# Attention scores as four 32-row matmul tiles into four shared PSUM banks, in place of one 96-row matmul on packed operands

## The reference

```python
xn = _layernorm(x, axis=-1)
x = x + attention(xn) + ffn(xn)

# attention: 16 heads of 16, segments of 512 rows, every 8th row is a key
qkv = einsum('bmd,ed->bme', x, Wqkv)              # q is scaled by hd ** -0.5
scores = einsum('bhspd,bhskd->bhspk', q4, k4)     # 512 queries x 64 keys in each segment
c = max(scores, over blocks of 64 queries)        # one value per key and block
w = exp(scores - c)
den = sum(w, axis=-1) + 1e-10
out = (w @ v4) / den ; out @ Wout.T

# ffn
h = relu(xn @ W1 + b1)                            # 256 -> 1024
y = h @ W2 + b2                                   # 1024 -> 256
```

## Time and profile before

| | |
|---|---|
| median of 3 runs | 1187.57 us (1187.46 to 1188.78) |
| span of the profiled execution | 1189.4 us, 22871 instructions |
| PE busy | 1162.9 us (98%) |
| DVE busy | 885.6 us (74%) |
| ACT busy | 657.1 us (55%) |
| POOL busy | 613.5 us (52%) |
| hardware DMA queue | 75376 packets, 101.90 MB |
| HBM read, written | 22.16 MB, 16.78 MB |

### The profile page before, as it was taken

The page is one execution under the profiler, slowest core; times in us unless marked ns, Lnnn a source line. Parts: engine busy times, 40 slices in busy tenths (PEclk is TensorE's granted clock), DMA queues, the critical chain, the costliest instruction groups (busy, mean ns, idle before and its releaser), DMA issues.

```text
span 1189.4 us, 22871 instructions
## 1 busy us (share of the span) xinstructions
PE 1162.9 (98%) x7457; PEld 955.7 (80%) x7457; DVE 885.6 (74%) x1437; ACT 657.1 (55%) x1142; POOL 613.5 (52%) x488
## 2 busy tenths in 40 slices
PE   5799999999999999999999999999999999999998
PEld 3578888888878888888888888888888888888888
DVE  7788777778787777777777787777877777777762
ACT  4545555565655565555565555556555555555653
POOL 2435654465554455554556544556544556544554
PEclk9889999999999999999999999999999999999999
DMA  5423343222333322333222433223343233332210
GB/s 184 99 73 93 85 106 100 63 82 70 101 101 84 80 72 81 98 106 84 68 81 75 106 101 84 72 70 88 101 106 82 56 87 84 106 102 55 67 49 36
DMA packets 75402, 102.24 MB, mean 86 GB/s; under 512 B 13808, under 2 KB 42096, under 8 KB 75376
## 3 DMA queue, kind: packets, MB, share of 16 engines
q1 hardware_dynamic: 75376, 101.90, 32.6%
HBM read 22.16 MB, written 16.78 MB: 33 GB/s over the span
## 4 chain that ended last, share of the span: by engine, by line
PE 96%; DVE 1%; issue 0%; SPq 0%; POOL 0%; DMA 0%; ACT 0%; DVEq 0%; POOLq 0%
PE y_bank L690 39%; PE h_bank L690 38%; PE misc L811 5%; PE s_bank L742 5%; PE misc L814 5%; PE misc L756 2%; PE misc L690 2%; PE misc L781 0%; PE misc L764 0%; DMA q_pack<-q_hi 0%; PE s_bank L690 0%; DVE w_exp L589 0%; DVE s_max L583 0%; DVE xn_keys L544 0%; DVE w_lo L506 0%
## 5 line engine op out<-in xcount | busy, mean ns | idle before, releaser
L338 POOL TENSOR_TENSOR h_lo<-h_full,h_hi 128x512 fp32r<-128x512 f32 x256 | 336.7, 1318 | 557.2 <-ACT h_full L403 553.3
L409 ACT ACTIVATE w_exp<-w_exp 128x512 f32<-128x512 f32 x256 | 162.7, 636 | 238.7 <-DVE w_exp L589 238.7
L690 PE MATMUL y_bank<-w_hi,h_hi 128*128 128x256 f32 x1024 | 290.6, 284 | 0.0
L690 PE MATMUL y_bank<-w_lo,h_hi 128*128 128x256 f32 x1024 | 290.5, 284 | 0.0
L690 PE MATMUL y_bank<-w_hi,h_lo 128*128 128x256 f32 x1024 | 290.2, 283 | 0.0
L596 DVE RECIPROCAL den<-den 128x256 f32<-128x256 f32 x128 | 222.3, 1739 | 39.9 <-ACT den L422 39.9
L401 ACT ACTIVATE h_hi<-h_bank,b_cols 128x512 fp32r<-128x512 f32 x256 | 176.1, 688 | 82.6 <-PE h_bank L690 76.8
L690 PE MATMUL h_bank<-xt_hi,w_hi 128*128 128x512 f32 x512 | 210.8, 412 | 1.9 <-DVE q_lo L611 1.9
L690 PEld LDWEIGHTS y_bank<-w_lo,h_hi 128*128 128x128 f32 x1024 | 196.0, 191 | 9.9
L690 PEld LDWEIGHTS y_bank<-w_hi,h_hi 128*128 128x128 f32 x1024 | 195.5, 191 | 9.3
L690 PE MATMUL h_bank<-xt_lo,w_hi 128*128 128x512 f32 x512 | 201.9, 394 | 0.0
(11 more groups left out here) (91 smaller groups left out, 1708.1 us busy)
## 6 DMA issues: line engine op xcount, KB each, us to landing
q_pack<-q_hi SPq DMA_DIRECT2D x256, 128.0 KB, 2.4
x_raw<-x SPq DMA_DIRECT2D x32, 512.0 KB, 3.3
q_pack<-q_lo SPq DMA_DIRECT2D x128, 128.0 KB, 2.4
out<-y SPq DMA_DIRECT2D x32, 512.0 KB, 2.9
k_pack<-k_hi SPq DMA_DIRECT2D x256, 32.0 KB, 1.9
k_pack<-k_lo SPq DMA_DIRECT2D x128, 32.0 KB, 1.9
x_keys<-x SPq DMA_DIRECT2D x16, 128.0 KB, 3.0
w_exp<-w SPq DMA_DIRECT2D x2, 1024.0 KB, 8.8
```

The source lines that it names most:

```text
L338: pool.tensor_tensor(h_part[1][:, i % HBUF], h_full[:, i % HBUF], f32(h_part[0][:, i % HBUF]), ALU.subtract).then_inc(h_lo, 1)
L409: act.activation(w_exp[:, pair], w_exp[:, pair], ACT.Exp).then_inc(w_ready, 1)
L690: mm = pe.matmul(ps, stationary[a], moving[b], start=start and c == 0 and n == 0, stop=stop and c == len(pairs) - 1 and n == 2, skip_group ...
```

## The change

The `misc` banks and the packed buffers go. There are four `s_bank`s, and they also hold the transposes of x (banks 0 and 1), keys and values (3 and 2), and weighted values (2 and 3 for the first four pairs, 0 and 1 for the others). Scores are made for four pairs at a time, in two groups in a step: four matmuls of 32 rows, one in each block of 32 partitions and each into its own bank, hi x hi, then four hi x lo, then four lo x hi, accumulating in PSUM. The order of the work on PE, ACT and DVE is changed to suit; POOL's is not touched.

```diff
-    PAIR_ORDER = [half * (PAIRS // 2) + j for j in range(PAIRS // 2) for half in range(DH)]
-    PACKED = 16 * 6
+    GROUP = PAIRS // DH
...
-        q_pack = sb("q_pack", [P, PAIRS, SEG], F32R)
-        k_pack = sb("k_pack", [P, PAIRS, P], F32R)
...
-        misc = [bank(f"misc{i}") for i in range(2)]
         h_bank = [bank(f"h_bank{i}") for i in range(2)]
-        s_bank = [bank(f"s_bank{i}") for i in range(2)]
+        s_bank = [bank(f"s_bank{i}") for i in range(GROUP)]
+        xt_bank = s_bank[0:2]
+        pv_bank = [s_bank[2:4], s_bank[0:2]]
+        key_bank = (s_bank[3], s_bank[2])
...
@@ sync: the whole of pack(s), with its 24 DMAs and their waits, goes @@
-                if norm:
-                    pack(s)
...
@@ scalar, step @@
                 for i in range(LAG, NH - 1):
-                    if i == 3 and norm and par == 0:
-                        keys_hi(s)
                     if attention:
                         exponential(s, i - LAG)
                     if i in first:
                         hidden(past(s), first[i])
                     if i == 5 and ffn:
                         attention_hi(s, 0, par)
+                if norm and par == 0:
+                    keys_hi(s)
                 if norm:
                     transposed_hi(s, par)
...
@@ vector, step @@
-                for n in range(PAIRS):
-                    if n == 0 and keys:
-                        normalise_keys(s + 2)
-                    if n == 4 and keys:
-                        drain_kv(s)
-                    if n == 5 and keys:
-                        mask_k(s)
-                    if n == 6 and norm:
-                        transposed_lo(s, par)
+                for n in range(GROUP):
                     if attention:
                         shift_scores(s, n)
-                    if n == 1 and norm:
-                        normalise(s + 2, par)
-                    if n == 1 and keys:
-                        keys_lo(s)
-                    if n in (2, 4) and ffn:
-                        invert_den(s, RP // QUADS + n // 2 - 1)
+                if keys:
+                    normalise_keys(s + 2)
+                if norm:
+                    normalise(s + 2, par)
+                if ffn:
+                    invert_den(s, 2)
+                for n in range(GROUP, PAIRS):
+                    if attention:
+                        shift_scores(s, n)
+                if keys:
+                    keys_lo(s)
+                if norm:
+                    transposed_lo(s, par)
+                if keys:
+                    drain_kv(s)
+                if ffn:
+                    invert_den(s, 3)
+                if keys:
+                    mask_k(s)
                 if norm:
                     finish_projections(s, par)
...
@@ tensor @@
-            def scores(s, n):
-
-                pair = PAIR_ORDER[n]
-                if n % 2 == 0:
-                    pe.wait_ge(pair_packed[n // 2], (s + 2) * PACKED)
-
-                pe.wait_ge(s_shifted, past((s + 1) * PAIRS + n - 1))
-                pe.matmul(s_bank[n % 2][:], k_pack[0:PR, pair], q_pack[0:PR, pair], start=True,
-                          stop=True).then_inc(s_psum, 1)
+            def scores(s, half, par):
+
+                pe.wait_ge(k_ready, s + 2 + par)
+                pe.wait_ge(k_hi, s + 2)
+                pe.wait_ge(k_lo, s + 2)
+                pe.wait_ge(q_hi, (s + 1) * DH + half + 1)
+                pe.wait_ge(q_lo, (s + 1) * DH + half + 1)
+                if half == 0:
+                    pe.wait_ge(num_ready, past((s + 1) * QUADS))
+                    pe.wait_ge(den_ready, past((s + 1) * QUADS))
+                else:
+                    pe.wait_ge(s_shifted, (s + 1) * PAIRS + GROUP)
+                for n, (a, b) in enumerate(((0, 0), (0, 1), (1, 0))):
+                    for j in range(GROUP):
+                        rows = slice(PW * j, PW * (j + 1))
+                        mm = pe.matmul(s_bank[j][:], k_part[a][rows, half], q_part[b][rows, half],
+                                       start=n == 0, stop=n == 2)
+                        if n == 2:
+                            mm.then_inc(s_psum, 1)
...
             def transpose_x(s, par):
                 pe.wait_ge(xn_ready, s + 3)
-                pe.wait_ge(num_ready, past((s + 1) * QUADS))
-                pe.wait_ge(den_ready, past((s + 1) * QUADS))
...
+                pe.wait_ge(s_shifted, past((s + 1) * PAIRS + GROUP + 2))
...
             def transpose_keys(s):
                 pe.wait_ge(xn_keys_ready, s + 4)
-                pe.wait_ge(den_ready, past((s + 1) * QUADS))
+                pe.wait_ge(s_shifted, past((s + 2) * PAIRS))
...
@@ weighted_values @@
-                if quad == 0 and norm:
+                if quad == 0 and norm and par == 0:
+                    pe.wait_ge(k_ready, s + 4)
+                if quad == 1 and norm:
                     pe.wait_ge(xt_lo, (s + 3) * DH)
-                else:
-                    pe.wait_ge(num_ready, (s + 1) * QUADS + quad)
-                    pe.wait_ge(den_ready, (s + 1) * QUADS + quad)
...
@@ tensor, step @@
                 if attention:
-                    scores(s, 0)
-                    scores(s, 1)
+                    scores(s, 0, par)
                 for i in range(LAG, NH):
-                    if i == 3 and norm and par == 0:
+                    if i == 4 and attention:
+                        scores(s, 1, par)
+                    if i == NH - 1 and norm and par == 0:
                         transpose_keys(s)
-                    if i == 5 and norm and par == 0:
-                        keys_values(s)
-                    if i == 6 and norm and par == 0:
-                        transpose_k(s)
                     if i == NH - 1 and norm:
                         transpose_x(s, par)
                     if i in first:
                         first_product(past(s), first[i], par if ffn else 1 - par)
-                    if attention and i > LAG:
-                        scores(s, i - 1)
                     if i in second:
                         second_product(past(s), second[i])
+                if norm and par == 0:
+                    keys_values(s)
                 if ffn:
                     second_product(s, NH - 2)
-                if attention:
-                    scores(s, NH - 1)
+                if norm and par == 0:
+                    transpose_k(s)
                 if norm:
                     for m in range(DH):
                         queries(s, par, m)
```

More of the change, by code:

```diff
@@ L171, in ln_attention_ffn @@
         q_lo = sem("q_lo")
-        pair_packed = [sem(f"pair_packed{j}") for j in range(PAIRS // 2)]
         v_ready = sem("v_ready")
@@ L271, in first_step @@
                 load_x(1, 1)
[L272 to L292, removed]
             def step(s, par, ffn, attention, norm, load):
@@ L406, in exponential @@
             def exponential(s, n):
-                pair = PAIR_ORDER[n]
                 act.wait_ge(s_shifted, (s + 1) * PAIRS + n + 1)
-                act.activation(w_exp[:, pair], w_exp[:, pair], ACT.Exp).then_inc(w_ready, 1)
+                act.activation(w_exp[:, n], w_exp[:, n], ACT.Exp).then_inc(w_ready, 1)
             def attention_hi(s, quad, par):
@@ L420, in attention_drain @@
                 act.wait_ge(att_ready, past(n - QUADS))
-                act.copy(num[:, quad], misc[0][:]).then_inc(num_ready, 1)
-                act.add(den[:, quad], misc[1][:], GUARD).then_inc(den_ready, 1)
+                act.copy(num[:, quad], pv_bank[quad][0][:]).then_inc(num_ready, 1)
+                act.add(den[:, quad], pv_bank[quad][1][:], GUARD).then_inc(den_ready, 1)
             def keys_hi(s):
@@ L435, in transposed_hi @@
                     act.wait_ge(xt_psum, (s + 2) * DH + c + 1)
-                    act.copy(xt[0][:, par, c], misc[c][:]).then_inc(xt_hi, 1)
+                    act.copy(xt[0][:, par, c], xt_bank[c][:]).then_inc(xt_hi, 1)
             def queries_hi(s, m):
@@ L517, in _ @@
             dve.wait_ge(k_mask_psum, 1)
-            dve.tensor_copy(k_mask[:], s_bank[1][:, 0:P]).then_inc(masks_made, 1)
+            dve.tensor_copy(k_mask[:], s_bank[2][:, 0:P]).then_inc(masks_made, 1)
             def statistics(s, par):
@@ L578, in shift_scores @@
             def shift_scores(s, n):
-                pair = PAIR_ORDER[n]
-                ps = s_bank[n % 2][:].rearrange("p (t n i) -> p t n i", t=T, n=NB)
+                ps = s_bank[n % GROUP][:].rearrange("p (t n i) -> p t n i", t=T, n=NB)
                 dve.wait_ge(s_psum, (s + 1) * PAIRS + n + 1)
-                dve.tensor_reduce(s_max[:, pair], ps.rearrange("p t n i -> p n t i"), AX.XY,
+                dve.tensor_reduce(s_max[:, n], ps.rearrange("p t n i -> p n t i"), AX.XY,
                                   ALU.max).then_inc(max_ready, 1)
@@ L587, in shift_scores @@
                 dve.wait_ge(max_ready, (s + 1) * PAIRS + n + 1)
```

(22 more changed lines are left out.)

20 lines of the change are left out of this document (7 added, 13 removed).

## The result

The changed kernel takes 1252.12 us (median of 4 runs, 1251.09 to 1252.59) against 1188.17 us for the kernel before (4 runs): ratio 1.054, 95% interval 1.0525 to 1.0555. It is slower, inside the range of 1200 to 1280 and 19 us above the 1233 that was forecast. The profiled execution has a span of 1250.8 us, 61.4 more than before, where the sum said 45.5.

A forecast was written before the change was run, and what follows sets the result against it. The prediction took PE's always busy stream as the bound. Its terms, +12.1 + 3 + 6 + 29 - 1.6 - 3 = +45.5 us, added to the median of 1187.57, gave 1233 us, 3.8% slower, range 1200 to 1280.

The forecast's parts named there:

- 64 groups at 1.11 for 256 matmuls at 0.23: On PE, groups of four row tiles replace the 96-row score matmuls, rounds plus mode edges: +12.1 us.
- (1): PE's second score group waits for four DVE shifts, nearly a tie: 0.1 us per step, +3 us in all.
- (2): In keys steps PE's transpose_keys waits for all eight DVE shifts, 0.4 us with the open load, 15 times: +6 us.
- (3): PE's last second_product waits for POOL's hidden_lo(7), queued behind attention_out(1), which waits for DVE's late fourth reciprocal: +29 us.
- one set of transposes less at an edge: In keys steps one fewer open weight load of 0.11 us behind transposes on PE, 15 times: -1.6 us.
- the start: At the kernel's start the 2.81 us wait for q_pack goes: 3 us saved, bounds 0 and 5.
- rival B: Weight loads of the row tiles follow one another on PE, group 1.84 us: 1271 us; chance 0.15.
- rival C: Row tiles on PE do not overlap at all: 1330 to 1355 us with edges and wait (3); chance 0.10.
- rival D: Wait (3) does not come, the reciprocal or POOL's two passes being quicker: 1204 us; chance 0.07.
- E: Packing traffic slows PE's reads, so matmuls speed up without it: at most 84 us, giving 1149; chance 0.04 for faster.
- rival A: The forecast itself: row tiles overlap, waits (1) to (3) come: 1233 us, own range 1213 to 1246; chance 0.60.

The follow-up runs named there:

- run 6: Changed kernel with fourth reciprocal directly behind the shifts and POOL's residual first, plus each group as four unpacked 96-row matmuls (output not the reference's): 1191.75 us.
- run 7: Changed kernel with fourth reciprocal directly behind the shifts and POOL's residual first, plus only the hi x hi round per score group: 1180.51 us.
- run 1: Changed kernel with invert_den(s, 3) on DVE moved up to directly behind the eighth shift: 1221.29 us.
- run 2: Changed kernel with POOL's queue alone changed, hidden_lo(7) ahead of attention_out(1): 1223.83 us.
- experiment 3: Changed kernel with POOL's residual (x_b) moved to the start of POOL's step: 1234.80 us.
- run 8: Changed kernel with fourth reciprocal directly behind the shifts and POOL's residual first, plus each group's matmuls ordered tile by tile: 1202.72 us.
- run 4: Changed kernel with normalise_keys on DVE moved ahead of the first shift, POOL as in the changed kernel: 1253.20 us.

## Why the prediction held, and where its sum was off

Step by step, on the span:

| term | forecast | measured |
|---|---|---|
| 64 groups at 1.11 for 256 matmuls at 0.23 | +12.1 | 1.10 each: +11.5 |
| (1) second group waits for four shifts | +3 | 0 |
| (2) transpose_keys waits for eight shifts | +6 | 14 waits of 1.26 in the stream: +18 |
| (3) second_product(7) waits for hidden_lo(7) | +29 | 29 waits, about 1.05 in plain steps and 1.13 in keys steps: +31 |
| one set of transposes less at an edge | -1.6 | 15 pairs of steps at -0.14 in run 6: -2 |
| the start, to the last y addition of step 0 | -3 | 93.0 against 90.7 us: +2.3 |
| sum | +45.5 | +61 by these terms, +61.4 on the span |

Right: that PE's stream is the time; that row tiles overlap like column tiles, and their loads too (rivals B and C fall with the group of 1.10); that 0.40 at the edges eats the gain of 4/4 over 3/4 of the array (runs 6 and 7); that the fourth reciprocal reaches PE through POOL's queue (runs 1 and 2, rival D falls); that ACT's lateness stays covered. E falls: plain matmuls still follow at 0.23 and 0.12.

That the time lies in the range is partly luck. The mechanism is that of rival A, but A's own range was 1213 to 1246, with bounds for (2) and (3) that the prediction does not give, and 1252 lies above it. The range reached to 1280 for rival B, which did not come true. And the steps were put at 36.4 and 38.2 us, while the terms of the sum give 36.5 and 38.5.

The term that is most mis-sized is (2), by 12 of the 16 us. It took 0.35 for xn_keys into a place where POOL's x_b runs. With T0 = 584.44, PE was ready at T0 + 16.2, as forecast (16.3), and the eighth shift ended at T0 + 17.4 in place of 16.6: xn_keys took 1.4 us more of DVE's time than its 0.35, and the other pieces together 0.6 less. So xn_keys alone makes the wait, and experiment 3 gives 17.3 us for moving x_b, the size of the whole measured term. The trace of before had warned. In its start, with POOL idle, the same four xn take 1.37 us, against 2.36 in the earlier trace rows:

```profile
30.33 1.37 DVE L574 TENSOR_SCALAR xn<-x_raw,mean_var,rstd 128x256 f32<-128x256 f32 x4
```

I took 0.35 for xn_keys as if POOL were idle, too, and did not ask why the two prices of xn differ. In the earlier trace rows the fourth xn runs into a hidden_lo of POOL and takes 1.40 us, the other three 0.41 each.

(3) is right to 2 us in all. It is too small by some 0.2 us in the keys steps (1.13 against 0.91): PE came to the wait at F + 7.22, not 7.33, and went on at F + 8.29, not 8.13 (F is 604.45 there).

The start is the second miss, by 5 us: 3 us were to be saved, and 2.3 are lost. The wait for the packed buffers is gone, but the timeline of the changed kernel shows, in step 0, a wait of the second group that the forecast had as a tie.

```profile
62.77 0.80 PE L724 MATMUL s_bank<-q_hi,k_hi 32*128 32x512 f32 x4 [5.61 <-DVE w_exp L558]
```

Run 6 shows that the row tiles are not the cause. How much belongs to the burst order and how much to the rest of the start was not separated, and the cause stays open.

## What to carry to other kernels

When small matmuls are packed into tiles, set what the rounds save against what the two changes of mode cost: here three rounds saved 0.23 us for 0.40 us of edges, and one 96-row matmul per pair was better. By these numbers two groups in a row would save 0.46 for the same edges; that is an estimate, and no run here has it. When an operation is moved on one engine, walk down the queue of every engine that waits for it: what cost 31 us was a ready instruction standing behind one that had become late. And the duration of a VectorE instruction, read from a trace, holds for its old neighbourhood: look at what GpSimd does at the new time.

## What the runs showed of the hardware

Row tiles were worked off as if they were separate streams: with the program's order tile by tile (run 8), the first matmuls of all four still started within 0.03 us, and the group took 602.71 - 601.59 = 1.12 us against 1.10. The Trainium skill (TensorE: Matmul & The Clock Gate, Part 3) says that matmuls start and end strictly in program order, with weight loads alone pulled ahead; across row tiles the trace of run 8 shows otherwise, and the measurement decides.

A tensor_scalar on DVE that started while a tensor_tensor of POOL ran did not get slower by a share, it ended only after the other had: 0.40 us became 1.88, with the end 0.15 us behind x_b's. In the changed kernel this holds for all 60 xn and xn_keys that began under x_b or a hidden_lo: each ends 0.148 to 0.155 us behind POOL's instruction, and with POOL idle they take 0.40 to 0.41 us. The Trainium skill (SBUF — State Buffer, Who interferes with whom) gives the rule: the port pair shared by the two engines is an exclusive lock, held for a whole instruction, and tensor_scalar can be of the kind that takes it. Runs 3 and 4 agree with it. DVE's k_lo, a tensor_tensor, behaves alike: in the changed kernel it begins under POOL's attention_lo and ends 0.28 us behind it, 1.19 us long on average against 0.54 before; PE did not wait for it.
